# A two-layer attention and FFN kernel: own slots for every link, an exclusive recurrence, own PSUM banks for two batches, weights quantised in the first attention

## The reference, cut to what matters

```
x = x + attn0(wkv(x, k, k, w0, u0, cond))   # RMS-normed heads, two softmaxes
x = x + ffn0 (wkv(x, k, k, w1, u1, cond))   # one fp8 matmul with per-tensor scales
x = x + attn1(wkv(x, k, k, w2, u2, cond))   # rotary, causal by blocks of 64, softmax
x = x + ffn1 (wkv(x, k, k, w3, u3, cond))   # ternary weights, int8 activations, relu squared

wkv(r, k, v, ...):   # runs over tokens in both directions
  ek = exp(min(k, 30));  ekv = ek * v
  fwd = scan(s*decay + ek), scan(s*decay + ekv);   bwd = the same in reverse
  den = fwd_ek + bwd_ek - ek + exp(min(u + k, 30))
  num = fwd_ekv + bwd_ekv - ekv + exp(min(u + k, 30)) * v
  return sigmoid(r) * num / max(den, 1e-8) * (0.8 + 0.2*tf)
```

## Time and profile before

| | |
|---|---|
| median of 3 runs | 409.94 us |
| profiled execution | 412.68 us |
| its span, first to last instruction | 410.9 us |
| VectorE (DVE) busy | 296.3 us, 72% |
| TensorE (PE) busy | 272.2 us, 66% |
| ScalarE (ACT) busy | 208.4 us, 51% |
| GpSimd (POOL) busy | 40.4 us, 10% |
| mean granted TensorE clock | 0.784 |

### The profile page before, as it was taken

How to read it: one execution, slowest core, us unless ns; L and a number is a source line. 1 busy time by engine, 2 the same in 40 slices (tenths; PEclk the granted TensorE clock), 3 DMA queues, 4 the chain that set the end, 5 groups by cost and what they waited for, 6 DMA issues and landing times.

```text
span 410.9 us, 5220 instructions
## 1 busy us (share of the span) xinstructions
PE 272.2 (66%) x1867; PEld 154.9 (38%) x1867; DVE 296.3 (72%) x536; ACT 208.4 (51%) x422; POOL 40.4 (10%) x61
## 2 busy tenths in 40 slices
PE   0142746448539767756766687979897997976745
PEld 0122413224314324424331335536464553633633
DVE  3998999999797995776398969694657337055761
ACT  5715695866874956171342136434466344232631
POOL 4110120200210114001000101010000000000000
PEclk9999757857856757895685689698699698595996
DMA  6200225346244252004123523565000000000001
GB/s 225 69 0 1 53 51 102 72 77 161 53 77 78 51 104 52 0 2 83 21 45 57 104 51 57 98 186 122 0 2 2 0 2 0 2 0 2 26 26 53
DMA packets 8089, 22.22 MB, mean 54 GB/s; under 512 B 1536, under 2 KB 2944, under 8 KB 7680
## 3 DMA queue, kind: packets, MB, share of 16 engines
q0 software_dynamic: 4032, 14.68, 19.0%
q1 hardware_dynamic: 4032, 7.21, 5.3%
HBM read 6.16 MB, written 1.05 MB: 18 GB/s over the span
## 4 chain that ended last, share of the span: by engine, by line
DVE 37%; PE 33%; issue 12%; ACT 11%; DMA 5%; POOL 0%; DVEq 0%; ACTq 0%; POOLq 0%
DVE fwd L656 5%; PE PM L1105 5%; PE PS L1222 4%; ACT E L498 3%; PE PS L1112 3%; PE PM L1053 3%; DVE kp L885 3%; DMA fwd<-bwd 3%; PE PO L1238 3%; PE PM L1166 2%; DMA fwd<-mid 2%; PE PM L1175 2%; DVE bwd L662 2%; PE PS L1284 2%; DVE rsum L759 2%
## 5 line engine op out<-in xcount | busy, mean ns | idle before, releaser
L885 DVE TENSOR_REDUCE kp<-PS 128x2 f32<-128x256 f32 x64 | 32.3, 549 | 17.8 <-PE PS L1199 17.7
L576 ACT ACTIVATE E<-PS 128x384 f32<-128x384 f32 x64 | 27.8, 488 | 29.8 <-PE PS L1222 29.8
L1112 PE MATMUL PS<-identb 128*128 128x512 bf16 x86 | 31.3, 452 | 16.2 <-ACT E L576 8.7
L498 ACT ACTIVATE E<-PS,negc,escale 128x256 f32<-128x256 f32 x64 | 35.2, 567 | 6.9 <-PE PS L1067 6.9
L1080 PE MATMUL PO<-E,vt 128*32 128x256 f32 x256 | 25.8, 540 | 13.0 <-DVE ytok L787 9.5
L1053 PE MATMUL PM<-ident,kp 128*128 128x128 f32 x128 | 24.4, 353 | 12.8 <-DVE kp L702 7.3
L1088 PE MATMUL PO<-ident,yc 128*128 128x128 f32 x64 | 17.4, 364 | 20.0 <-ACT yc L473 19.9
L490 ACT ACTIVATE E<-PS,negc,escale 128x1024 f32<-128x1024 f32 x16 | 19.2, 1200 | 20.2 <-PE PS L1067 20.2
L1067 PE MATMUL PS<-TP 32*128 32x256 f16 x256 | 21.3, 344 | 8.5 <-DVE TP L714 6.1
L1053 PEld LDWEIGHTS PM<-ident,kp 128*128 128x128 f32 x128 | 19.4, 182 | 18.1 <-issue 9.3
L307 POOL DMA_DIRECT2D fwd<-mid x14 | 12.2, 871 | 132.4 <-DVE fwd L656 132.4
(11 more groups left out here) (179 smaller groups left out, 616.7 us busy)
## 6 DMA issues: line engine op xcount, KB each, us to landing
fwd<-mid POOLq DMA_DIRECT2D x14, 512.0 KB, 4.5
fwd<-bwd POOLq DMA_DIRECT2D x14, 512.0 KB, 4.5
kT<-in_kT SPq DMA_DIRECT2D x4, 256.0 KB, 4.3
xT<-in_xT SPq DMA_DIRECT2D x4, 256.0 KB, 6.2
G<-in_attn SPq DMA_DIRECT2D x1, 1024.0 KB, 4.9
ek<-in_w SPq DMA_DIRECT2D x1, 1024.0 KB, 5.2
ekv<-in_w SPq DMA_DIRECT2D x1, 1024.0 KB, 9.4
out<-mid SPq DMA_DIRECT2D x8, 128.0 KB, 1.7
```

Source lines behind the costliest of these rows:

```text
L498: nc.scalar.activation(E[:, p % 4, i, v * T:(v + 1) * T], PS[:, 2 + i, v * T:(v + 1) * T], ACT.Exp, bias=negc[:], scale=escale[:], accum_o ...
L576: nc.scalar.activation(E[:, p % 4, i, 0:384], PS[:, i, 0:384], ACT.Exp, scale=QSCALE).then_inc(S["e1_done"], 1)
L885: nc.vector.tensor_reduce(kp[:, b % 2, u * H + 2 * j:u * H + 2 * j + 2, D], PS[:, at0:at0 + 2, lo:hi], AX, ALU.max, negate=True).then_inc( ...
L1112: nc.tensor.matmul(bank, identb[:], identb[:, None, :].broadcast_to([P, 4, P]), start=True, stop=True)
```

## The change

1. Every link of every batch gets a slot of its own, in a table per engine's helper (PROJ0, SQUARE0, ..., ROTARY, V_COPY, Q_COPY, K_COPY, KT_COPY). `rms` and `normed` are each split in two.
2. Each of the six parts of a recurrence step gets a slot of its own (STEP). Only step 0 sums on VectorE. Steps 10 to 15 lie at other places; the last gate comes at slot 27 instead of 12. mid and bwd become rings of two, fwd stays a ring of three.
3. The reverse scan becomes exclusive: it yields the sum without the token's own term, by adding first and multiplying after, over ek and ekv shifted by one element. The subtraction of ek in `inputs` goes. vf of batches 1 to 3 moves to ScalarE.
4. `v_rows` on POOL goes: the values stay unscaled in kp, and the gain g3 is applied in the yT copy.
5. For batch 0 of the second attention q is turned into PS banks 0 and 1, k into PS banks 2 and 3, q with its maximum row into PO; V of batches 0 and 1 is projected into PO.
6. The weights of the last FFN load at the start, and are summed, scaled, rounded and made bf16 integers by ScalarE during the first attention; VectorE only clamps.

```
+            for tile in (ek, ekv):
+                nc.gpsimd.memset(tile[:, 0:N + B + 1:SEG + 1], 0.0).then_inc(S["ek_edge"], 1)
...
-        EARLY = 2
-        WKV0 = {4 * i: EARLY + i for i in range(PAIRS)}
-        WKV1 = {-18: 10, -12: 11, -6: 12, -2: 13, 2: 14, 5: 15}
+        EARLY = 1
+        STEP = {1: (None, None, None, None, 2, 2),
+                2: (None, None, 0, 2, 6, 7),
+                3: (3, 4, 5, 6, 10, 11),
...
+                8: (23, 24, 25, 26, 32, 33),
+                9: (27, 28, 29, 30, 42, 42),
+                10: (43, 43, 43, 45, 53, 54),
+                11: (54, 56, 58, 59, 64, 63),
+                12: (62, 64, 65, 68, 71, 72),
+                13: (67, 69, 70, 70, 76, 77),
+                14: (72, 72, 73, 74, 79, 80),
+                15: (76, 77, 78, 79, 83, 85)}
+        PREPARE, INPUTS, AHEAD, BEHIND, LN, GATE = range(6)
...
+        TURN_Y0 = (14, 22, 29, 38)
+        YT0 = (14, 23, 30, 38)
+        PROJ_OUT0 = (14, 23, 32, 38)
+        WEIGHT_ABS = (0, 4)
+        WEIGHT_ROUND = (13, 20)
+        WEIGHT_INT = (15, 24)
+        CLAMP = (6, 8)
+        AT_QK = (-16, -14, -2, 7)
+        AT_V = (-15, -14, 0, 9)
+        AT_Q = (-15, -9, 2, 11)
+        AT_K = (-15, -7, 3, 12)
+        QRE = (-3, 6, 13, 21)
+        ROTARY = ((-16, -14, -1, 8), (-16, -14, 0, 9))
+        GATED2 = (None, -15, -2, 6)
+        SQUARE = (26, 28, 32, 33, 37, 38, 43, 44)
+        TANH3 = (17, 24, 32, 38)
+        SLOTS1 = range(-2 * PAIRS - 1, B * PAIRS + 17)
+        FIRST1 = SLOTS0 - SLOTS1[0]
...
+        def v_bank(b):
+            return PO[:, 0, :] if b < 2 else PM[:, 0, :]
+
+        def q_banks(b):
+            return PS[:, 0:2] if b == 0 else PM[:]
+
+        def k_banks(b):
+            return PS[:, 2:4] if b == 0 else PM[:]
...
-                nc.vector.scalar_tensor_tensor(mid[:, r, 0], mid[:, r, 0], EXP30, ek[:, seg(b)], ALU.min,
-                                               ALU.subtract).then_inc(S["m_done"], 1)
+                m = mid[:, pair_at(n)]
+                nc.vector.tensor_scalar(m[:, 0], m[:, 0], EXP30, None, ALU.min).then_inc(S["m_done"], 1)
...
+                if n >= 2 + EARLY:
+                    dve.wait_ge(S[f"back_added{(n - 2) % RING}"], added(n - 2))
+                nc.vector.tensor_tensor_scan(bwd[:, pair_at(n), i][:, ::-1], src[:, padded(b, 1)][:, ::-1],
+                                             DT[n % 2][:, 1:SEG + 1][:, ::-1], 0.0, ALU.add,
+                                             ALU.mult).then_inc(S["scan_done"], 1)
...
+            def weight_abs(n):
+                act.wait_ge(S[f"ld_w{n + 1}"], 16)
+                nc.scalar.activation(G[2][:, :], (w1f, w2f)[n], ACT.Abs,
+                                     accum_out=wsc[:, n:n + 1]).then_inc(S["wabs_done"], 1)
+
+            def weight_int(n):
+                act.wait_ge(S["wround_done"], n + 1)
+                nc.scalar.activation((w1q, w2q)[n], (w1f, w2f)[n], ACT.Copy, bias=-ROUND).then_inc(S["wint_done"], 1)
```

More of the change, by code:

```diff
@@ L252, in due, with steps @@
+        def v_bank(b):
[4 more added lines that the diff above has]
+            return PS[:, 2:4] if b == 0 else PM[:]
         def due(slots, p):
             return [i for i, at in enumerate(slots) if at == p]
+        def steps(p, part):
+            return [n for n, at in STEP.items() if at[part] == p]
         def hid_bank(t):
@@ L336, in _ @@
             nc.gpsimd.memset(ones[:], 1.0).then_inc(S["pads_set"], 1)
-            pool.wait_ge(S["gains_done"], 1)
-            v_rows(0)
-            for p in range(B * PAIRS):
-                if p % PAIRS == 4 and p // PAIRS + 1 < B:
-                    v_rows(p // PAIRS + 1)
-                for n in steps0(p, 0):
+            nc.gpsimd.memset(vt[:, :, :, D:2 * D], 1.0).then_inc(S["v_ones"], 1)
+            wkv(1)
+            for p in range(SLOTS0):
+                for n in steps(p, AHEAD):
                     wkv(n)
             pool.wait_ge(S["ktr0_done"], B)
-            pool.wait_ge(S["v0_done"], B)
             half = slice(0, P // 2), slice(P // 2, P)
@@ L436, in _, with square0 @@
             prepare(2)
-            def rms(b):
+            for b in range(1, B):
+                nc.scalar.activation(vf[:, seg(b)], kT[:, seg(b)], ACT.Copy, scale=fb[:, b:b + 1]).then_inc(S["vf_done"], 1)
+            def square0(b):
                 act.wait_ge(S["proj0_done"], b + 1)
@@ L818, in _ @@
                     group_out(p // 2 - 3)
-                if j == 0 and b + 1 < B:
-                    gated(0, b + 1)
-                if j == 2 and b + 1 < B:
-                    normed(b + 1)
-                if j == 0 and b >= 2:
-                    residual("out0_done", b - 1, 0, b - 2)
-                for n in steps0(p, 7):
-                    gate(n)
-                wkv(steps0, p)
+                for n in steps(p, GATE):
+                    gate(n)
+                for bb in due(GATED0, p):
+                    gated(0, bb)
+                for bb in due(RESIDUAL0, p):
+                    residual("out0_done", bb + 1, 0, bb)
+                wkv(p)
+                for bb in due(SQUARES0, p):
+                    squares(bb)
+                for bb in due(NORMED0, p):
+                    normed(bb)
                 if p == 2:
@@ L983, in final @@
                                                ALU.mult, ALU.add).then_inc(S["res_done"], 1)
-            inputs(10)
-            for i in range(2):
-                ahead(10, i)
             for p in SLOTS1:
@@ L1043, in project0, with turn @@
                 ins.then_inc(S["proj0_done"], 1)
-            def turn(b, first, done, wait):
+            def turn(b, first, done, wait, into=PM):
                 for s, n in wait:
@@ L1389 @@
     gcol[:, 1, :, 2] = -1.0
+    gcol[..., 3] = A(L0_attn_g3)
     data = {
```

464 lines of the change are left out of this document (240 added, 224 removed).

## The result

Before: 409.77 us (median; 406.87 to 409.94). After: 355.5 us (352.56 to 358.08). The ratio is 0.867 (95% interval 0.858 to 0.875): 54 us faster, where 40 were forecast. The forecast was 370, its range 354 to 390: the result lies 1.5 us inside the range's lower end. The profiled execution of after took 352.56 us (span 350.6) at a mean granted clock of 0.907, that of before 412.68 at 0.784.

A forecast was written before the change was run, and what follows sets the result against it. Three limits: VectorE's work in the first attention, a chain of waits in the entry, TensorE's work in the second attention. 8.5 + 4.5 + 26 + 2 = 41 us off 412.7 gives 371.7, about 369 against the median; predicted 370, range 354 to 390.

The forecast's parts named there:

- First attention and its end: First attention: 8.5 us gained from less VectorE work; its end: 4.5 us from moved transfer wait, logarithm and projection.
- nothing of either is waited for before slot 2: Start: step 1's two transfers on POOL's queue and the early memset of vt's ones hold up nothing before slot 2.
- VectorE's busy sum: Sign over the whole kernel: VectorE's total busy time falls by about 20 us.
- Rival A: First attention: ScalarE, 90% full with its added passes, takes over; the 8.5 us gain is lost, 378.5 us; chance 0.14.
- Entry: Entry to the second attention, up to slot 2: 26 us faster; 11 us if TensorE stays at its lower clock.
- queued behind both turns and three ScalarE copies because all used PM: Entry: cause given for the second project_qk coming late before the change, with VectorE idle 10.51 us.
- Slots 2 to 31: Second attention: removed work and added scans, preparations and table loads nearly balance; 2 us faster, bounds 15 faster, 12 slower.
- The rest: The FFN's tail after the second attention: no change, 0 us.
- has the same operations: nothing: FFN's tail: its operations are unchanged, so no time is gained or lost.
- D: Second attention, slots 0 to 21: ten scan pairs delay TensorE and lower its clock, 5.5 to 7.5 us each; chance 0.04.
- B: Entry to the second attention stays at TensorE's lower clock: 15 us less gain, 385 us; chance 0.07.
- C: Second attention pays for its table changes and added passes: 14 us less gain, 384 us; chance 0.12.

The follow-up runs named there:

- a_memsets_early: The kernel after, with POOL's kp memsets ahead of its wait for the condition's Tanh and those of ones and vt behind step 0's first product: 349.4 us.
- a_recur_old: The kernel after, with steps 10 to 15 of the recurrence back at their old places, banks and everything else new: 369.5 us.
- a_stalls: The kernel after, with two more VectorE scans (2.4 us) ahead of the maxima of slots 4, 9, 15 and 20 of the second attention: 362.7 us.

## Why the prediction was right, and where not

**Sum.** The mechanisms were mostly those named, the total was 14 us short, and most of that is one term. That the result still fell inside the range is partly luck: it did so by 1.5 us, and the sum, made against the profiled execution, said 371.7 where after's profiled execution took 352.56, which is below the range.

**First attention and its end: 13 forecast, 8.8 measured, 12.7 without the wait for the memsets (a_memsets_early).** The two-input operations run at 0.69 again: L686, the successor of L631 in the earlier trace rows, has a mean of 684 ns. The plain minimum takes 0.44 us in steps 1 to 15, as forecast. What failed is the step on POOL's work at the start, "nothing of either is waited for before slot 2": the minimum of step 0 waited for the memsets, 4.1 us, a term that the sum did not have. It is also what VectorE's busy sum lacks to the 20 us forecast (15.6 measured). That ScalarE's passes are mostly hidden held: at most 4 of 12 us show. Rival A's "90% full" was nearly so (97.4 of 114.7 us, VectorE 99.4), but the 8.5 us it put at stake were not lost.

**Entry: 26 forecast, 29.4 measured.** From project_qk to slot 2 by the prediction's mark it took 41.3 us, forecast 43. The size was right and its split was not, so it is in part luck. The step that failed is "queued behind both turns and three ScalarE copies because all used PM": the banks are worth 1.5 to 3.4 us. The recurrence's steps are worth 19.1, more than VectorE's 13 us. With them ahead of the rotary VectorE first waits 3.43 us for ScalarE's preparation, TensorE stands 7.4 us before the first turns, which then take 3.57 instead of 1.94 us, and it waits 2.28 and 2.44 us between the maxima. In before VectorE waited 2.01 us at that place, so a_recur_old has 1.4 us of wait that before had not.

**Slots 2 to 31: 2 forecast, 16.2 measured, the mis-sized term.** I set the 7 us taken from VectorE and ScalarE's 4 against 12 us of scans that come in, with preparations and table loads, and called it even. Undone one by one: the weight work is worth 11.0 us in before (8 by the medians, and a part of it, two clamps, is still in after), the separate slots of rotary, copies and squares 6.3, the FFN's places 6.2 (squares in both). The steps that came in cost 7.2 (a_recur_old), and all of it behind slot 17, with four scans, the late logarithms and their table loads: up to there five scans more (6 us) cost nothing that shows. That sums to 16.3, close to the 16.2 measured, but the squares are counted twice and the parts were measured in two kernels, so the agreement is no proof. The table loads were seven and not five here, and three of them cost 4.9 us up to slot 22; by the one-per-pair count they were underpriced. Eleven loads in all, where nine were named. No gap stood behind a load of 1.28 us.

**The rest: 0 forecast, 5.8 measured.** The step that says the FFN's tail "has the same operations: nothing" failed: the old places cost 8.0 us in the one execution traced, 2.2 more than the term. The same work in another order is not the same time on a chain of five engines' hand-overs.

**Rivals.** D (scan pairs of VectorE hold TensorE and lower the clock, 5.5 to 7.5 us each) did not happen: the steps that came in cost 7.2 us together. Its price per pair was met once, nearly: of the four pairs of a_stalls one cost 5.4, the others 0 to 3. B did not happen: 0.96. C named real costs, but its 14 us were not lost: the slots became faster.

## What to carry to other kernels

Cost an item of work not by its length but by what stands in its slot: 8 us of VectorE's weight work that sat between the maxima and TensorE (with 4 us of ScalarE's) cost 8 to 11, 12 us of passes on an engine with slack cost at most 4, and 13 us of VectorE's recurrence steps moved out of a bare entry into busy slots were worth 19 there and cost 7 in the slots. Look also at which engine an item of work waits for: one that is moved ahead brings its wait along (3.43 us here). When an operation's form changes (two tensors to one), look again at everything that runs beside it. Undo parts singly before crediting the most visible one: the own banks looked like the cause of the entry and were not.

## What the runs showed of the hardware

- A one-tensor minimum of VectorE (0.43 us alone) took 4.54 us beside four consecutive memsets of GpSimd; the two-tensor form took 0.69 beside the first of them.
- A logarithm and an exponential behind a Tanh got a table load each (1.28 + 1.28 us); with the set that holds both loaded ahead, one load served the pair and the next pairs. The Trainium skill, ScalarE: Activation LUTs, section Table sets: the hidden batching unit, says that both functions are in one set and need one load; the trace agrees only where that load is asked for.
- TensorE's granted clock was 0.72 in an entry with waits of 6.31, 2.12 and 3.28 us and 0.96 in one whose longest was 2.67; sixteen turns took 3.9 us at the lower level (1.2 GHz) and 1.94 at the upper (2.4 GHz).
- Four VectorE insertions of 2.44 us each cost TensorE's chain 0, 3, 3 and 5.4 us; behind the last, eight score matmuls took 1.65 us instead of 0.92.
